# Routing scores from one premultiplied, split matrix, and the last pair's values turned by TensorE

## What is computed

```python
q = (hidden_states @ Wq).reshape(b, t, 2, H, RET // 2)
sim = jnp.einsum('btphn,hkpn->pbthk', q, keys)
sc, ix = jax.lax.top_k(sim, KPH)
```

```python
mem = _split_heads(memories @ Wm)
k = jnp.concatenate([k, mem], axis=2)
v = jnp.concatenate([v, mem], axis=2)
out = jnp.einsum('bhij,bhjd->bhid', jax.nn.softmax(dots, axis=-1), v)
```

## Time and profile before

| | us |
|---|---|
| median of 3 runs | 2101.09 |
| lowest and highest run | 2097.49, 2103.79 |
| the profiled execution | 2102.5 |
| its span, first to last instruction | 2100.7 |
| PE busy in the span | 2011.8 |
| DVE busy | 1227.2 |
| ACT busy | 888.6 |
| mean granted TensorE clock | 0.982 of full |

### The profile page before, as it was taken

How to read it: one execution, slowest core, us unless ns; L and a number is a source line. 1 busy time by engine, 2 the same in 40 slices (tenths; PEclk the granted TensorE clock), 3 DMA queues, 4 the chain that set the end, 5 groups by cost and what they waited for, 6 DMA issues and landing times. The chain is left out here.

```text
span 2100.7 us, 34732 instructions
## 1 busy us (share of the span) xinstructions
PE 2011.8 (96%) x14294; PEld 1448.5 (69%) x14294; DVE 1227.2 (58%) x2054; ACT 888.6 (42%) x2081; POOL 61.0 (3%) x78
## 2 busy tenths in 40 slices
PE   7999998899999999989999999899999999969999
PEld 6864555588868888834447788677777777754687
DVE  6446688553347888899998210554453544437563
ACT  4234442443233333689995332332332332333342
POOL 0000000000000000200000000000000000000122
PEclk9999999999999999999999999999999999989999
DMA  6310000122110111020003245645354454453001
GB/s 263 94 35 0 1 2 2 58 64 66 36 47 21 60 41 61 22 99 21 0 1 121 82 121 159 170 137 139 86 146 112 125 135 113 125 161 98 1 1 40
DMA packets 117084, 161.10 MB, mean 77 GB/s; under 512 B 11312, under 2 KB 77360, under 8 KB 116464
## 3 DMA queue, kind: packets, MB, share of 16 engines
q1 hardware_dynamic: 116928, 158.89, 25.4%
HBM read 110.23 MB, written 15.07 MB: 60 GB/s over the span
## 5 line engine op out<-in xcount | busy, mean ns | idle before, releaser
L1272 ACT ACTIVATE R<-bank 128x512 f32<-128x512 f32 (+3 forms) x151 | 89.3, 598 | 393.1 <-PE bank L949 310.4
L1538 ACT ACTIVATE R<-R 128x64 f32<-128x64 f32 x896 | 217.3, 345 | 3.3 <-DVE R L2241 3.3
L949 PE MATMUL bank<-cth,wmh 128*128 128x512 f32 x512 | 209.7, 410 | 6.1 <-DVE ctl L2339 3.9
L949 PE MATMUL bank<-ctl,wmh 128*128 128x512 f32 x512 | 203.0, 397 | 0.0
L949 PE MATMUL bank<-cth,wml 128*128 128x512 f32 x512 | 202.4, 395 | 0.0
L526 PE MATMUL bank<-XN,arena 128*128 128x512 f32 x320 | 146.1, 608 | 0.0
L949 PEld LDWEIGHTS bank<-cth,wmh 128*128 128x128 f32 x512 | 96.9, 189 | 42.2 <-issue 12.3
L526 PE MATMUL bank<-Y,arena 128*128 128x512 f32 x256 | 115.9, 598 | 1.7 <-ACT H L1581 1.7
L949 PEld LDWEIGHTS bank<-cth,wml 128*128 128x128 f32 x512 | 96.8, 189 | 22.6
L949 PEld LDWEIGHTS bank<-ctl,wmh 128*128 128x128 f32 x512 | 97.0, 189 | 20.2
L526 PEld LDWEIGHTS bank<-XN,arena 128*128 128x128 f32 x320 | 60.5, 195 | 70.6 <-issue 70.2
(11 more groups left out here) (430 smaller groups left out, 4192.4 us busy)
## 6 DMA issues: line engine op xcount, KB each, us to landing
Y<-value_turn SPq DMA_DIRECT2D x256, 128.0 KB, 2.6
H<-in_ctxT SPq DMA_DIRECT2D x30, 512.0 KB, 5.2
arena<-in_L_attn_mlp_w SPq DMA_DIRECT2D x8, 1024.0 KB, 5.3
R<-value_rows SPq DMA_DIRECT2D x32, 132.0 KB
arena<-in_L_ffn_Wg SPq DMA_DIRECT2D x4, 1024.0 KB, 7.1
arena<-in_L_ffn_Wu SPq DMA_DIRECT2D x4, 1024.0 KB, 5.2
arena<-in_L_ffn_Wd SPq DMA_DIRECT2D x4, 1024.0 KB, 5.7
arena<-in_downT SPq DMA_DIRECT2D x4, 1024.0 KB, 6.3
```

The costliest lines, as they stand in the source:

```text
L949: last = mm(b[:, :].rearrange("p (a c) -> p a c", a=2), w_, c_[:, k, :, :], start=(k == 0 and n_ == 0), stop=(k == 3 and n_ == 2))
L1272: fn(dst, src, ACT.Copy).then_inc(act_bank_free, 1)
L1538: last = fn(into[:, x // 2, h, :, x % 2], RC["Ey"][:, t, h, :], ACT.Copy, scale=RC["Ex"][:, t, h, 8 * j + x:8 * j + x + 1])
```

## The change

Three things change.

- **Scores.** `Wq` is passed transposed (`wqT`), and loaded with `key_blocks` between the loads of the second and the third MLP weight block, behind a wait for `x_low` (the splits of the first MLP's input, after which `XN` is free). During the up product of the second MLP quarter (j = 1), `key_weights(k)` multiplies the two after each o: four plain products of 128 columns into a DVE bank. ACT copies the bank into `sim_high`, DVE subtracts into `sim_low`. The routing stage then needs no queries: each score block of 128 tokens is the split product of the features with this matrix, twelve f32r products of 512 columns. The two arrays take no new room (they lie where `value_turn` and `dp_high_odd` lie).
- **Features.** ACT copies the feature banks straight to `y_high`, and DVE subtracts it from the bank into `y_low` and frees the bank. The plain `Y` is not written there any more. For the first half DVE's part stands ahead of the end of the stage.
- **Last pair.** `value_blocks` turns the memory rows by PE, 16 transposes of 128 x 128 for each batch into four DVE banks, after the scores of that batch, and DVE copies the banks into `RD["vt"]` (`values`). The four block turns and the 16 transfers of this pair are gone, and with them the wait for `values_full` on PE. The other 15 pairs stay.

```diff
+            def key_weights(k):
+                if k == 0:
+                    pe.wait_ge(S["c_wq"], 16)
+                    pe.wait_ge(S["c_kb"], 16)
+                b = open_dve(("simw", k))
+                for i in range(4):
+                    last = mm(b[:, tl(i)], CWQ[:, i, tl(k)], key_blocks[:, i, :], start=True, stop=True)
+                last.then_inc(dve_bank_full, 1)
...
                     if c == C2 - 1:
                         piece_used[piece_no[(("b1", j), o)]] = (act_bank_full, UA.n)
+                        if j == 1:
+                            key_weights(o)
...
-            pe.wait_ge(S["c_wq"], 16)
             for c in range(C2):
-                normed(pe, 2, c)
-                for o in range(4):
-                    if (o, c) == (3, 0):
-                        features(2, 1)
-                    b = open_act(("cq", o, c))
-                    linear(b[:, :], CWQ, tl(o), Y, ch(c)).then_inc(act_bank_full, 1)
-            on_act(("cq", 3, C2 - 1))
-            pe.wait_ge(S["c_kb"], 16)
-            for t in range(TT):
-                b = open_act(("sim", t))
-                for j in range(4):
-                    last = mm(b[:, tl(j)], H[:, 0, j, tl(t)], RC["kb"][:, j, :], start=True, stop=True)
-                last.then_inc(act_bank_full, 1)
-            pe.wait_ge(S["x_low"], 5 * C2)
+                if c:
+                    features(2, 1)
+                four = [open_act(("sim", 4 * c + i)) for i in range(4)]
+                for k in range(4):
+                    on_act(("feat", 2, c, k))
+                    for i in range(4):
+                        t = 4 * c + i
+                        for n, (y_, w_) in enumerate(((y_high, sim_high), (y_low, sim_high), (y_high, sim_low))):
+                            last = mm(four[i][:, :], y_[:, k, tl(t)], w_[:, k, :], start=(k == 0 and n == 0), stop=(k == 3 and n == 2))
+                        if k == 3:
+                            last.then_inc(act_bank_full, 1)
...
+            def value_blocks(bb):
+
+                for blk in range(2):
+                    for half in range(2):
+                        b = open_dve(("vt", bb, blk, half))
+                        for o in range(4):
+                            last = nc.tensor.transpose(b[:, tl(o)], kts[bb // 2 % 2][:, 4 * half + o, bb % 2, 128 * blk:128 * blk + 128],
+                                                       tab("ident"))
+                        last.then_inc(dve_bank_full, 1)
...
-                if i == 0:
+                if i == 0 and bb // 2 < PAIRS - 1:
                     pe.wait_ge(values_full, 256 * (bb // 2 + 1))
...
                 attention_scores(b0)
+                if pr == PAIRS - 1:
+                    value_blocks(b0)
...
                 attention_scores(b1)
+                if pr == PAIRS - 1:
+                    value_blocks(b1)
...
+                        if j == 1:
+                            act.wait_ge(dve_bank_full, UV.at[("simw", o)] + 1)
+                            fn(sim_high[:, o, :], UV.banks[UV.at[("simw", o)] % 4][:, :], ACT.Copy).then_inc(S["c_simw"], 1)
...
-            features(2, 0)
+            def features_high(c):
+                for k in range(4):
+                    fn(y_high[:, k, ch(c)], unit(("feat", 2, c, k))[:, :], ACT.Copy).then_inc(S["x_high"], 1)
+
+            features_high(0)
             end_stage()
...
             for c in range(C2):
-                for o in range(4):
-                    if (o, c) == (3, 0):
-                        features(2, 1)
-                    copy_out(H[:, 0, o, ch(c)], unit(("cq", o, c))[:, :])
-            for c in range(C2):
-                fn(y_high[:, :, ch(c)], Y[:, :, ch(c)], ACT.Copy).then_inc(S["x_high"], 1)
-            for t in range(TT):
-                copy_out(RC["sim"][:, t, :], unit(("sim", t))[:, :])
+                if c:
+                    features_high(1)
+                for t in range(4 * c, 4 * c + 4):
+                    copy_out(RC["sim"][:, t, :], unit(("sim", t))[:, :])
...
+                        if j == 1:
+                            dve.wait_ge(S["c_simw"], o + 1)
+                            v.tensor_tensor(sim_low[:, o, :], unit(("simw", o))[:, :], sim_high[:, o, :].bitcast(f32),
+                                            ALU.subtract).then_inc(dve_bank_free, 1)
...
+            def features_low(c):
+                for k in range(4):
+                    dve.wait_ge(S["x_high"], 4 * C2 + 4 * c + k + 1)
+                    v.tensor_tensor(y_low[:, k, ch(c)], UA.banks[UA.at[("feat", 2, c, k)] % 4][:, :],
+                                    y_high[:, k, ch(c)].bitcast(f32), ALU.subtract).then_inc(act_bank_free, 1)
+
+            features_low(0)
             end_stage()
...
             second_half(2)
-            for c in range(C2):
-                dve.wait_ge(S["x_high"], 4 * C2 + c + 1)
-                v.tensor_tensor(y_low[:, :, ch(c)], Y[:, :, ch(c)], y_high[:, :, ch(c)].bitcast(f32), ALU.subtract
-                                ).then_inc(S["x_low"], 1)
+            features_low(1)
...
+            def values(bb):
+                for blk in range(2):
+                    for half in range(2):
+                        b = unit(("vt", bb, blk, half))
+                        v.tensor_copy(RD["vt"][:, 2 * (bb % 2) + blk, :, 128 * half:128 * half + 128].rearrange("p a (o n) -> p o a n", o=4),
+                                      b[:, :].rearrange("p (o a n) -> p o a n", o=4, a=4)).then_inc(dve_bank_free, 1)
...
-                turn_values(pr)
+                if pr < PAIRS - 1:
+                    turn_values(pr)
+                else:
+                    dve.wait_ge(values_full, 256 * pr)
+                    dve.wait_ge(dve_bank_full, UV.at[("pv", 2 * pr - 1)] + 1)
+                    values(b0)
                 maxima(b1)
+                if pr == PAIRS - 1:
+                    values(b1)
...
-            sp.wait_ge(S["x_low"], 4 * C2)
-            sp.dma_start(CWQ, rows4("L0_ffn_Wq")).then_inc(S["c_wq"], 16)
+                if loads[i][0] == ("b1", 1):
+                    sp.wait_ge(S["x_low"], 4 * C2)
+                    sp.dma_start(CWQ, rows4("wqT")).then_inc(S["c_wq"], 16)
+                    sp.dma_start(key_blocks, dram["key_blocks"]).then_inc(S["c_kb"], 16)
...
             sp.wait_ge(stage_done, 4 * 3)
-            sp.dma_start(RC["kb"], dram["key_blocks"]).then_inc(S["c_kb"], 16)
...
-                move_values(pr)
+                if pr < PAIRS - 1:
+                    move_values(pr)
```

More of the change, by code:

```diff
@@ L128, in perceiver @@
                                        for n_ in ("dp_high_odd", "dp_low_odd"))
+        with ExitStack() as until_last:
+            sim_high, sim_low = (until_last.enter_context(nc.sbuf_tensor(n_, [128, 4, 512], f32r)) for n_ in ("sim_high", "sim_low"))
         value_turn = sb("value_turn", [128, 4, 4, 256])
@@ L261, in perceiver @@
             "b_ckln", "b_clock", "b_gsp", "b_gcs", "b_gcp", "b_pdif", "b_pexp", "b_sq", "b_rn", "b_cos",
-            "a_khi", "a_qhi", "a_whi", "a_wlo", "a_chi", "a_clo", "a_nm", "a_xn", "a_ahi", "a_ctx", "c_topin", "c_topexp", "c_p", "c_kb", "c_fac", "c_ee", "c_mul", "c_y", "c_wq",
+            "a_khi", "a_qhi", "a_whi", "a_wlo", "a_chi", "a_clo", "a_nm", "a_xn", "a_ahi", "a_ctx", "c_topin", "c_topexp", "c_p", "c_kb", "c_fac", "c_ee", "c_mul", "c_y", "c_wq", "c_simw",
             "w_high", "w_low", "x_high", "x_low", "h_high", "h_low",
@@ L370, in perceiver @@
                      ("out", (8, 128)), ("rg", (1, N)), ("cw", (4, 16)), ("t", (2, N)), ("pm", (1, 32)), ("lg", (1, N))])
-        RC = region([("sim", (8, 512)), ("kb", (4, 128)), ("count_tab", (8, 64)), ("Ex", (8, PH, 32)), ("rank_tab", (8, 256)),
+        RC = region([("sim", (8, 512)), ("spare", (4, 128)), ("count_tab", (8, 64)), ("Ex", (8, PH, 32)), ("rank_tab", (8, 256)),
                      ("Ey", (8, PH, 64)), ("eq", (1, 2048)), ("s", (4, 512)), ("xv", (1, 8)),
@@ L377, in perceiver @@
         CWQ = XN[:, 2:4].rearrange("p a b -> p (a b)").rearrange("p (k n) -> p k n", k=4)
+        key_blocks = R[:, 17408:17408 + 512].rearrange("p (j n) -> p j n", j=4)
         hid_raw = R[:, 16384:16384 + 1024].rearrange("p (i n) -> p i n", i=2)
@@ L2775 @@
           "L0_attn_gate_w", "L0_attn_p_w", "L0_attn_out_w", "L0_attn_clock_w", "L0_attn_mlp_w1", "L0_attn_mlp_w2",
-          "L0_ffn_Wg", "L0_ffn_Wu", "L0_ffn_Wd", "L0_ffn_Wq", "L1_xattn_Wq", "L1_xattn_Wkv",
+          "L0_ffn_Wg", "L0_ffn_Wu", "L0_ffn_Wd", "L1_xattn_Wq", "L1_xattn_Wkv",
           "L1_xattn_Wm", "L1_xattn_Wo", "L1_attn_Wc", "L1_attn_Wd"]
@@ L2812, in layouts @@
     got["key_blocks"] = kb
+    got["wqT"] = np.ascontiguousarray(a["L0_ffn_Wq"].T)
     def paired(rows):
```

## The result

The changed kernel takes 2077.86 us (median of 4 runs, 2074.42 to 2081.56) against 2102.4 us for the kernel before (4 runs, 2097.49 to 2103.79): a ratio of 0.9895, with an interval of 0.9877 to 0.9914. That is 22 us less, 18 to 26 by the interval; forecast were 18.6.

What follows compares the result with a forecast made beforehand. PE was taken to bound the kernel (busy 2011.8 of 2100.7 us), with latencies setting the last pair. Gains of 7.9 (routing stage) and 10.7 us (last pair) sum to 18.6, off the median 2101.09: 2082.5 us, range 2077 to 2091.

Steps and rivals of the forecast that it cites:

- Score products, 21.5 us: Routing stage: 96 f32r products of 512 columns at 0.224 us each take 21.5 us on PE.
- rival 3: Routing stage: score products miss the f32r distance, deciding from 0.418 us; kernel slower, 2144 us; chance 2%.
- Wait in the middle, 2.0 us: Routing stage, between score halves: PE waits 2.0 us for the last of four banks, freed by DVE; bounds 1.0 to 3.0.
- Rival 2: Routing stage: the middle wait is 3.0 us and the clock falls behind it; gain 14 us, 2087; chance 8%.
- Part 1 in sum, 7.9 us: Routing stage with key matrix: 29.9 us in place of 37.8, a gain of 7.9 us, bounds 6 and 9.5.
- Weighted sums 6.8 us earlier: Last pair: by a walk over DVE's and PE's work, PE's weighted sums start 6.8 us earlier.
- Pauses in the sums: Last pair: SP's weight loads, suspected of the 2.78 us pause, finish by about 1860 us, so 0.59 us is kept.
- The clock, 1.5 us of price: Last pair: upper clock level for token transposes, half the low-clock price for the rest, 1.5 us off the 12.2 us gain.
- Part 2 in sum, 10.7 us: Last pair of the cross attention: `output` starts earlier, a gain of 10.7 us, bounds 7 to 12.2.
- Rival 1: Last pair: SP's early loads slow PE's instruction supply, clock stays low; gain there 5 us, 13 in all, 2088; chance 12%.
- Rival 4: Last pair: DVE's copies out of turned blocks cost twice the price, only the scores change pays; 2093; chance 5%.
- Rival 5: Whole kernel: the forecast holds as worked out, within 2078 to 2087 us; chance 73%.

Runs made afterwards that it cites:

- changed_loads_late: The changed kernel with SP's large weight loads held until the last weighted sum is done; 2079.39 us, ratio 0.9921 to the kernel before.
- pair_alone: The kernel before with only the last pair's change (values turned by TensorE), routing stage as before; 2084.68 us, ratio 0.9941.
- changed_again: The changed kernel itself run once more, unaltered, against the kernel before; 2077.63 us, ratio 0.9905.
- scores_alone: The changed kernel with the last pair's turns and transfers as before, leaving only the scores change; 2092.27 us, ratio 0.9967 to the kernel before.

## Why the prediction was right

The forecast of 2082.5 us lies 4.6 us above the measured median, which is inside the stated range of 2077 to 2091, though by only 0.9 us, and 0.1 us below the 2078 to 2087 given to the forecast as worked out; its sum of 18.6 us lies inside the intervals of both timings. Step by step:

- **Removed, 37.8 us.** The whole stage went, as worked out.
- **Key matrix, 3.6 us.** 3.6 by the four blocks, 0.22 us for each product, and the switch between plain and split products cost nothing, as taken.
- **Score products, 21.5 us.** 22.0. The distance is 0.227 in most of the run and 0.23 to 0.30 for the first of each half; the second MLP quarter gave 0.224. Mis-sized by 0.5. This also ends rival 3, which wanted over 0.418.
- **Start of the stage, 1.0 us.** From the start of the last row turns to the first score product are 3.19 us (591.18 to 594.37), where they were 2.33 to the first query product (589.50 before to 591.83): 0.86.
- **Wait in the middle, 2.0 us.** 2.15 us, released by `y_low`, as worked out; its end at 609.17, and not at 607.38, shows that it hung on the four banks opened at once. Rival 2 had 3.0 us and a fall of the clock behind the wait. The wait was 2.15 us in all five profiles with this bank order. The fall came in one of them, changed_loads_late (rows above), and cost 1.6 us. So half of rival 2's mechanism exists, and the two profiles of the changed kernel happen not to have it: what is right here is in part luck.
- **Transposes, 1.75 us.** 605.37 to 609.43 is 4.06 us, less the wait 1.91: 0.16 more.
- **Part 1 in sum, 7.9 us.** 0.86 + 22.0 + 1.91 + 2.15 = 26.9 for the new stage, 30.5 with the key matrix, a gain of 7.3. What is short by 0.6 is nearly all in the product's distance. Timed alone 7.0 us. The MLP was to start near 621.7; it started at 620.43 and 621.83 in the two profiles, the first with 1.9 us that arose ahead of the change.
- **Weighted sums 6.8 us earlier.** 7.05. Each step fits. Moved by the 14.03 us between the two starts of b0's scores, the first copies end at 1847.97 (1848.0 forecast), the last copies of turned probabilities at 1854.6 (1854.8), the tail at 1855.1 (1855.3), and the sums start at 1855.9 (1856.1).
- **Pauses in the sums.** The suspect was right: held loads take the pause away. Their time was right too: the large ones of the earlier trace rows were issued from 1830.2 us on, which is 1844.2 on the clock of before, and the DMA share is down to 0.14 by 1845.5 to 1846 (1860 on that clock). But this isn't ahead of the second half of the weighted sums, which started at 1843.5, and a pause of 0.50 us fell into it, where 0.59 was kept. That the size fits is luck: the 0.59 came from the end of a pair's sums, a pause of another kind, which doesn't go with the loads.
- **The clock, 1.5 us of price.** This step was wrong in its reason. I wrote that the change leaves no PE idle long enough, and that the upper level would hold for the token transposes and mostly beyond. For the token transposes it did (1.75 us). But it fell at 1844.4 with no pause of PE over 0.8 us in the 6 us before, while PE ran transposes and 64-column products, and the cost was real: the last 16 transposes took 3.68 us, not 1.75, the second half of the sums about 1.2 us more, `output` 14.47 and not 13.83 us. That is 1.9 + 1.2 by my terms ahead of `output`, of which DVE hides a part, and 0.6 behind it. So the gain at `output`'s start was 9.9 us in this profile, 11.1 in pair_alone and 11.3 in changed_again, about the 10.7 taken. In changed_again the clock fell only at 1849.1, for 3.4 us, and the last 16 transposes still took 3.4 us. The price had about the right size for a wrong reason.
- **Part 2 in sum, 10.7 us.** 9.9 to 11.3 by the traces, 12.4 (8 to 16) timed. The kernel before pays for the clock in this stretch as well: its low-clock time from the last pair into `output` adds up to 13.7 us, that of scores_alone to 23.9 us, against 3.4 to 10.2 us in the profiles of the changed forms, and the mean clock is 0.982 and 0.981 against 0.984 to 0.988. But this is already in the distances: before's last low spell ends at 1876.9, ahead of `output` at 1877.21, and only 1.7 us of those of scores_alone and 1.4 us of the changed kernel's lie behind the start of `output`. So it doesn't explain a timed gain above the traced distance. That difference is smaller than the interval, and stays open.

In the changed kernel's last pair the clock fell amid transposes and short products with hardly a pause; in the kernel before it rose while PE ran transposes alone. So the runs bear out neither that idle time alone decides nor that transposes alone keep the clock down. The page TensorE: Matmul & The Clock Gate of the Trainium skill, PE-mode transpose, holds that transposes don't count as busy in the same way as other work for the clock; the trace after speaks for it more than the trace before, which the prediction set against it, and the two together leave it open.

- **Rivals.** Rival 1 wanted new pauses beside the loads and a gain of 5 us in part 2: the interval of pair_alone excludes 5 us, though its mechanism came in small: a pause of 0.50 us beside the loads, which the prediction had named as a sign of being wrong, and 10 us of low clock in one profile. Rival 4 wanted DVE's permuted copies at double price: they take 2.49 us for four, the same as plain ones. Rival 5, the forecast as worked out, holds in its terms, and its 2078 to 2087 is missed by 0.1 us.

The sum of 18.6 stands against 17.2 and 18.6 by the traces' own distances and 19.9 and 22 timed. It has no term for low-clock spells outside the two places, and these differ by some us between executions.

## What to carry to other kernels

Turn with TensorE where TensorE would stand still for the transfer, and nowhere else: the same 32 transposes and eight copies brought 12 us in the last pair (11 in the trace) and cost 5 us in the trace in the one before it. Price products by the distance between their starts in a full stretch, and a stretch set by latencies as a walk over every engine's queue; the first came out within 0.6 us of 7.9, the second within 0.3 us of each step up to the sums. When several banks are opened at once, the last one's release is the wait; filling them one by one took it from 2.15 to 0.16 us. And when a wait is removed, look at who is busy without a gap behind it (here DVE): moving its work forward only moves the wait.

## What the runs showed of the hardware

- TensorE paused for 2.78 and 2.75 us inside 192 small products, with nothing in the profile that it waited for, with large weight loads in flight and the DMA share at 1.00 to 1.05; with these loads held there was no such pause. What links the two isn't shown. Lighter pauses of 0.6 to 1.5 us at the end of a pair's sums are there with and without those loads.
- In the changed kernel the granted clock fell to 0.50 for 10 us after TensorE had been busy 5.11 of 6.00 us and had paused for no more than 0.8 us at once, in a stretch of transposes and products of 64 columns. In another execution of the same kernel the low spell there was 3.4 us.
- With the clock at 0.50, f32r products of 512 columns started 0.43 us apart, and 0.227 us at 1.00 (changed_loads_late).
- A DVE copy from a bank of 512 columns into a place permuted by blocks of 32 costs the same as a plain one (0.6 us from start to start, four in 2.49 us).
- A plain product of 128 columns among split ones of 512 costs 0.22 us, as much as one of those, and the switch is free.
